# A graph network kernel on one core: TensorE's dense chunks also wait for GpSimd's gathers

## The chip, the core and the metric

One core of a Trainium2 chip. The metric is device microseconds of one execution; lower is better. The core's engines run their own instruction queues in order and meet only in semaphores: TensorE (PE) multiplies, VectorE (DVE) and ScalarE (ACT) work elementwise, GpSimd (POOL) here issues the gathers, SyncE (SP) and ScalarE issue the other transfers.

## What is computed

There are 6250 nodes with 64 features and 200,000 edges, sorted by destination, each with a source, one of 32 types and a weight. The first layer sends `x[src]` through one of 32 matrices that are mixed from 4 bases, scales by the edge's weight and sums by destination; then come a bias, relu, the addition of `x` and a layernorm. The second layer does nearly the same with one matrix, a self loop and a division by the summed weights.

```python
msg_b = jnp.einsum('ei,bio->ebo', h[src], weight)      # 4 bases
msg = jnp.einsum('ebo,eb->eo', msg_b, w_comp[etype]) * edge_norm[:, None]
x = layernorm(x + relu(segment_sum(msg, dst, N) + bias))
h = x @ W                                              # second layer
out = segment_sum(deg_inv[dst] * ew * h[src], dst, N)  # with loops of weight 1
x = layernorm(x + out + b)
```

## The kernel before

**Steps.** The edges are cut into 1563 chunks of 128. A *step* takes a group of 8 chunks; three steps (`U`) make an iteration, there are 65 iterations (`ITERS`), so 195 steps, and a tail of 3 chunks. All is unrolled on TensorE; on GpSimd it is a loop.

**First layer, in each step.** GpSimd issues one indirect transfer for each chunk (L824): 128 rows of `x`, one to a partition, into one of three buffers `gathered_rows`. In the function `gather_group` (L815) it first waits until ScalarE has written the group's indices (`idx_ready`) and counts `gathers_begun` up. ScalarE writes these indices (L927) when TensorE has read the rows that lay in the same buffer, so three steps back (`rows_read`). TensorE multiplies the rows with small factors (`sum_parts`, L1283), ScalarE copies the result (L985), and TensorE places it in a window of 44 nodes (L1296). Eight times in the first 20 iterations SP fetches the last chunk's rows instead of GpSimd, so there are 1559 gathers of `x`.

**Second layer, beside it.** The second layer isn't gathered. For each iteration of 24 chunks TensorE builds a *dense block*: how much each source node contributes to a window of destinations. `sum_chunk` (L1249) is one dense chunk: three matmuls of one-hot matrices with the "main" part (L1259) and three with the seam to the next chunk (L1269), into four banks in turn (`dense_ps`, `node_ps`, `types_ps`, `sums_ps`). It waits for VectorE's one-hots (`hots_ready`; made at L1886 to L1897) and for ScalarE's copies of the banks (`chunk_copied`, L1056), and it counts `dense_summed`. The blocks are stored in memory (SP, L733), come back when nodes of the first layer are finished (`load_unit`, L632), and TensorE applies them: to the last block at once (L1349), to earlier ones in "visits" (L1383), late ones in runs of three (L1406).

**TensorE's order in a step S**, from iteration 5 (L1480 on): dense chunks 0 and 1; the sum of the rows of step S-2, behind their landing (L1283); dense chunks 2, 3, 4; the placing of S-2 (L1296); dense chunks 5, 6, 7; in each third step the block products (L1349); the visits (L1383, none to six a step, more in later iterations); the coefficients for VectorE (L1244).

**What already holds GpSimd.** From iteration 8 on (step 24) a gather group is called with `behind_dense`. Then its third, fifth and seventh gather (`GATHERED_BEHIND = {2: 5, 4: 8, 6: 9}`) wait for dense chunks: for five of the step before, for all eight of it, and for the first of its own step. After each of these three waits GpSimd counts `gathers_paced` up. Both counts, `gathers_begun` and `gathers_paced`, are there before the change; nobody waits for them.

**After the loop** TensorE runs the last visits, some of which stand in its queue ahead of the last groups' sums, transforms the last batch of nodes and finishes the second layer (L1431), and the results are normalised and stored.

A second version of everything, for inputs that don't fit the planned order, is in the program and isn't run.

Of the kernel before, what the change touches and what calls it, by code (L numbers as in the profile page):

```python
# [36 lines left out]
U = 3  # L37
# [59 lines left out]
FETCHES = 4  # L97
# [114 lines left out]
def gnn_two_layers(nc, x, src, dst, etype, eweight, w0, w_comp, bias0, w1, bias1, out):  # L212
# [17 lines left out]
    with ctx:  # L230
# [158 lines left out]
        for u, (b, k, end, with_partial) in enumerate(UNITS):  # L389
            if u < BEGUN[-1]:  # L390
                step = next(n for n in range(ITERS * U) if BEGUN[n + 1] > u)
# [767 lines left out]
        def _(pe):  # L1159
# [77 lines left out]
            def look_up_coefs(step, s, chunks, count, halves=None):  # L1237
# [8 lines left out]
                if 4 * h + n == chunks:  # L1246
                    last.then_inc(coefs_ready, count)

            def sum_chunk(b, h, j):  # L1249

                n = b * DENSE + j
                pe.wait_ge(hots_ready, n + 2)
                if j == 0 and b:
                    pe.wait_ge(chunk_copied, n)
                values = NODES_OF[j] * TILES
                main = dense_ps[j % 4][:, 0:values]
                seam = dense_ps[(j + 1) % 4][:, 0:TILES]
                for w in range(3):
                    last = nc.tensor.matmul(main, lo_hot[:, w, j // 2, :, j % 2], node_hot[:, j // 2, 0:values, j % 2],  # L1259
                                            start=(j == 0 and w == 0), stop=(w == 2), skip_group_check=True)  # L1260
                    if w == 0 and (j == LAST_BANK or b == 0 and j < LAST_BANK):

                        nc.tensor.matmul(dense_ps[j % 4][:, values:values + TILES], no_node[:, :], no_node[:, 0:TILES],
                                         start=False, stop=True, skip_group_check=True)
                last.then_inc(dense_summed, 1)
                if j < DENSE - 1:
                    pe.wait_ge(chunk_copied, n + 1)
                    for w in range(3):
                        nc.tensor.matmul(seam, lo_hot[:, w, j // 2, :, j % 2], carry_hot[:, j // 2, :, j % 2],  # L1269
                                         start=(w == 0), stop=(w == 2), skip_group_check=True)  # L1270
# [163 lines left out]
            with pe.If(early == 1):  # L1434
# [42 lines left out]
                for i in range(FIRST_REGULAR, ITERS):  # L1477
# [3 lines left out]
                    for s in range(U):  # L1481
                        step = i * U + s
                        j0, of_last = DENSE_OF[s].start, divmod(step - 2, U)
                        mixed = i < MIXED_UNTIL
                        for j in range(j0, j0 + (1 if mixed else 2)):
                            sum_chunk(i, i, j)

                        if taken and s == 0:
                            pe.wait_ge(self_added, 2 * taken)
                        if turns is not None and s == 1:  # L1490
                            pe.wait_ge(nodes_read, turns + 1)
                        if turned is not None and s == 2:
                            pe.wait_ge(self_added, 2 * turned + 1)
                        if mixed:
                            for v in range(CH - 1):
                                between(i, s, v)
                                sum_chunk(i, i, j0 + v + 1)
                        else:
                            sum_rows(*of_last, step % 2)
                            for j in range(j0 + 2, j0 + 5):  # L1500
                                sum_chunk(i, i, j)
                            if i >= MANY_FROM:
                                pe.wait_ge(unit_added, BEGUN[step])
                            place(*of_last, step % 2)
                            for j in range(j0 + 5, j0 + CH):
                                sum_chunk(i, i, j)

                        use_coefs(step)
                        if s == 2 and tiles_done(i - 1):
                            pe.wait_ge(partial_taken, i)  # L1510
                        if s == 1 and tiles_done(i - 1):
                            apply_block(i - 1, i - 1)
                        for u in range(BEGUN[step], min(BEGUN[step] + VISITS_OF_COEFS, BEGUN[step + 1])):
                            sum_unit_of_block(u, visit_ps[u - BEGUN[step]])
                        if mixed:
                            look_up_coefs(step, s, CH, 1, [1])
                        else:
                            look_up(i, s)
                        if i >= MANY_FROM:
                            pe.wait_ge(window_added, step - 1 + FREE)  # L1520
                        for u in range(BEGUN[step] + VISITS_OF_COEFS, BEGUN[step + 1]):
                            sum_unit_of_block(u, visit_ps[u - BEGUN[step]])
                        if turns is not None and s == 0:
                            pe.wait_ge(window_added, (i - 1) * U + 1 + FREE)
                            transform(0, turns, parts_ps)
                        if turned is not None and s > 0:
                            turn_x1(turned, s - 1, parts_ps, 1)
# [873 lines left out]
```

## Time and profile before

| | us |
|---|---|
| median of 3 runs | 2767.2 |
| lowest, highest | 2765.88, 2772.87 |
| span of the profiled execution | 2042.2 |
| TensorE busy | 1497.4 |
| GpSimd busy | 1495.6 |
| VectorE busy | 1288.6 |
| ScalarE busy | 856.8 |

The span goes from the first to the last instruction of one profiled execution. The profiled execution's own time is not recorded; the median of the runs lies 725.0 us above its span. Busy times are by engine; matmuls overlap their weight loads.

### The profile page before, as it was taken

Reading aid. Unit: us, or ns where it says so; the run is one execution under the profiler, and the core shown is the slowest. Engines: PE = TensorE matmul, PEld = TensorE weight load, DVE = VectorE, ACT = ScalarE, POOL = GpSimd, SP = SyncE. Lnnn points to the kernel's source line nnn. Section 1 sums busy time; section 2 is a strip of 40 time slices with the busy share of each in tenths; the row PEclk is TensorE's granted clock in tenths of the full one; section 3 lists DMA queues with packets and bytes.
Section 4 is the critical chain, followed back from the end, with each engine's and each line's share of the span. In section 5 each row is a group of like instructions: output and inputs, shape, how many; then the busy total and the mean of one; then the engine's idle time right before and its main releaser. Section 6 shows DMA issues by size and latency. Waiting matters only on the chain.

```text
span 2042.2 us, 61156 instructions
## 1 busy us (share of the span) xinstructions
PE 1497.4 (73%) x21470; PEld 1196.1 (59%) x21470; DVE 1288.6 (63%) x3623; ACT 856.8 (42%) x2171; POOL 1495.6 (73%) x1590
## 2 busy tenths in 40 slices
PE   3785566655765776777677687778778788888986
PEld 2554444544554655566566566566667667677854
DVE  8886555756557555666655575565765656477647
ACT  5563343534444443444344344443444434344313
POOL 7777777777777777777777777777777777777750
PEclk7898777878787888888888898899999999899998
DMA  5544434434334455445444545554355554455695
GB/s 135 156 148 149 141 103 142 140 128 134 92 128 140 121 152 156 147 128 152 142 121 136 147 107 160 148 151 142 105 155 157 165 163 110 122 179 141 198 346 187
DMA packets 197569, 299.93 MB, mean 147 GB/s; under 512 B 66502, under 2 KB 137083, under 8 KB 191135
## 3 DMA queue, kind: packets, MB, share of 16 engines
q1 hardware_dynamic: 99496, 167.96, 23.3%
q0 software_dynamic: 50112, 51.41, 12.9%
q10 hardware_dynamic: 47671, 76.76, 12.4%
q8 instruction: 173, 2.83, 0.6%
q14 instruction: 117, 0.96, 0.1%
HBM read 187.43 MB, written 108.56 MB: 145 GB/s over the span
## 4 chain that ended last, share of the span: by engine, by line
PE 33%; POOL 29%; issue 19%; DMA 9%; DVE 3%; ACTq 3%; ACT 2%; DVEq 1%; POOLq 1%
POOL gathered_rows L824 29%; DMA gathered_rows<-in_x,idx 8%; PE coefs_ps L1383 4%; PE types_ps L1259 4%; PE coefs_ps L1349 3%; PE node_ps L1259 3%; PE sums_ps L1259 3%; PE sums_ps L1283 3%; PE dense_ps L1259 3%; PE sums_ps L1296 3%; ACTq L648 2%; ACT room L1056 1%; PE node_ps L1269 1%; PE sums_ps L1360 1%; PE coefs_ps L1244 1%
## 5 line engine op out<-in xcount | busy, mean ns | idle before, releaser
L824 POOL DMA_INDIRECT gathered_rows<-in_x,idx x1559 | 1475.7, 947 | 477.5 <-issue 426.7
L1283 PE MATMUL sums_ps<-gathered_rows,chunk_factors 128*32 128x64 f32 x3118 | 98.3, 253 | 407.0 <-DMA gathered_rows<-in_x,idx 218.7
L1897 DVE TENSOR_TENSOR first_room<-first_room,dve_ps 128x1024 bf16<-128x1024 bf16 x585 | 365.0, 679 | 0.0
L1283 PEld LDWEIGHTS sums_ps<-gathered_rows,chunk_factors 128*32 128x32 f32 x3118 | 63.1, 125 | 423.2 <-issue 208.6
L1056 ACT COPY room<-dense_ps 128x294 f32 x390 | 168.8, 433 | 332.1 <-PE dense_ps L1259 277.5
L985 ACT COPY parts<-sums_ps 128x128 f32<-128x128 f32 x196 | 52.0, 265 | 465.6 <-PE sums_ps L1283 462.3
L1919 DVE TENSOR_TENSOR dve_ps<-coefs_ps,edges 128x32 f32<-128x32 f32 x196 | 38.6, 197 | 330.7 <-PE coefs_ps L1244 326.2
L1259 PE MATMUL dense_ps<-first_room 128*128 128x245 bf16 x1170 | 219.2, 301 | 31.8 <-DVE first_room L1897 31.6
L1056 ACT COPY room<-node_ps 128x294 f32 x390 | 168.8, 433 | 168.1 <-PE node_ps L1259 61.8
L1891 DVE TENSOR_TENSOR first_room<-dve_ps,first_room 128x1960 bf16<-128x1960 f16 (+2 forms) x260 | 238.7, 939 | 0.0
L1259 PE MATMUL sums_ps<-first_room 128*128 128x245 bf16 (+1 forms) x1170 | 233.8, 312 | 0.0
L1259 PE MATMUL types_ps<-first_room 128*128 128x245 bf16 x1170 | 227.5, 311 | 0.0
L1259 PE MATMUL node_ps<-first_room 128*128 128x245 bf16 x1170 | 211.9, 293 | 0.0
L1056 ACT COPY room<-sums_ps 128x294 f32 (+1 forms) x390 | 171.4, 439 | 70.9 <-ACT room L1056 49.3
L1056 ACT COPY room<-types_ps 128x294 f32 x390 | 168.9, 433 | 69.5 <-ACT room L1056 47.0
L1976 DVE TENSOR_TENSOR acc_room<-acc_room,sums_ps 128x88 f32 x196 | 47.6, 243 | 238.1 <-PE sums_ps L1296 227.3
L1383 PE MATMUL coefs_ps<-acc_room,x_nodes 128*64 128x107 f32 x2742 | 170.6, 260 | 0.0
L1383 PEld LDWEIGHTS coefs_ps<-acc_room,x_nodes 128*64 128x64 f32 x2742 | 143.7, 136 | 15.3 <-issue 9.5
L1349 PE MATMUL coefs_ps<-room,x_nodes 128*64 128x107 f32 x2632 | 136.5, 258 | 7.5 <-ACT x_nodes L996 5.7
L1269 PEld LDWEIGHTS node_ps<-carry_hot,first_room 128*128 128x128 bf16 x1170 | 87.7, 106 | 87.1 <-ACT room L1056 70.9
L1269 PE MATMUL node_ps<-carry_hot,first_room 128*128 128x49 bf16 x1170 | 101.7, 196 | 46.2 <-ACT room L1056 45.0
L1886 DVE TENSOR_TENSOR first_room<-dve_ps,first_room 128x1024 bf16<-128x1024 f16 x195 | 133.1, 683 | 2.6 <-PE dense_ps L1259 1.4
(300 smaller groups left out, 2470.4 us busy)
## 6 DMA issues: line engine op xcount, KB each, us to landing
acc_room<-block_table ACTq DMA_DIRECT2D x147, 374.5 KB
block_table<-room SPq DMA_DIRECT2D x11, 2621.5 KB
type_rows<-in_edge_type SPq DMA_DIRECT2D x260, 96.0 KB
gathered_rows<-in_x,idx POOLq DMA_INDIRECT x1559
block_table<-room SPq DMA_DIRECT2D x9, 2247.0 KB
block_table<-room SPq DMA_DIRECT2D x9, 1872.5 KB
block_table<-room SPq DMA_DIRECT2D x10, 1498.0 KB
acc_room<-block_table ACTq DMA_DIRECT2D x43, 321.0 KB
```

Of the source, the lines that this page charges most:

```text
L824: pool.indirect_dma_start(gathered_rows[:, s, j, 0:D], None, rows, bass.IndirectOffsetOnAxis(ap=idx[:, s, j:j + 1], axis=0)).then_inc(rows ...
L985: nc.scalar.copy(parts[:, q, :, :], parts_ps[:, 0:QUADS * D].rearrange("p (k f) -> p k f", f=D)).then_inc(part_copied, count)
L1056: nc.scalar.copy(blocks_out[:, h % 2, :, bass.ds(offset, nodes)], dense_ps[j % 4][:, 0:nodes * TILES].rearrange("p (w h) -> p h w", h=TILE ...
L1259: last = nc.tensor.matmul(main, lo_hot[:, w, j // 2, :, j % 2], node_hot[:, j // 2, 0:values, j % 2], start=(j == 0 and w == 0), stop=(w = ...
L1269: nc.tensor.matmul(seam, lo_hot[:, w, j // 2, :, j % 2], carry_hot[:, j // 2, :, j % 2], start=(w == 0), stop=(w == 2), skip_group_check=True)
L1283: last = nc.tensor.matmul(parts_ps[lane:lane + LANE, D * k:D * k + D], chunk_factors[:, q, c, :], rows, start=True, stop=True)
L1296: last = nc.tensor.matmul(window_ps[D * h:D * h + D, 0:HALF * WIN], parts[:, q, k, :], places[:, q, k, HALF * h:HALF * h + HALF, :].rearra ...
L1349: last = nc.tensor.matmul(partial_ps[side:side + D, :], x_nodes[:, t, 1:D + 1], blocks_out[:, h % 2, t, :], start=(t < 2), stop=(t >= done ...
L1383: last = nc.tensor.matmul(to[side:side + D, :], x_nodes[:, FIRST_TILE[k] + t, 1:D + 1], tile_of(u, t), start=(not with_partial and t < 2), ...
L1886: nc.vector.tensor_tensor(lo_hot[:, 2, q0:q1, :, :], compared(P), keys(lo_key, P), ALU.is_equal).then_inc(lo_hots_ready, 1)
L1891: nc.vector.tensor_tensor(node_hot[:, a:e, 0:values, :], key_iota[:, 0:values, :].unsqueeze(1).to_broadcast([P, e - a, values, 2]), of_pai ...
L1897: last = nc.vector.tensor_tensor(lo_hot[:, w, q0:q1, :, :], lo_hot[:, 2, q0:q1, :, :], part_of_weights(w), ALU.mult)
```

## The change

Before each dense chunk, TensorE now also waits for GpSimd. `v` is the chunk's number in its step, and `step` in the new function is the step before the chunk's own. Chunks 0 and 1 wait until the gather group of the step before has been begun, chunks 2 and 3 until that group's third gather has been let go, chunks 4 and 5 until its fifth, chunks 6 and 7 until its seventh. This holds from step 25 on, since the counts of `gathers_paced` begin at step 24. GpSimd's own waits stay as they are.

```diff
+            def wait_for_gather(step, v):
+
+                if step >= 2 * FETCHES * U:
+                    if v > 1:
+                        pe.wait_ge(gathers_paced, 3 * (step - 2 * FETCHES * U) + v // 2)
+                    else:
+                        pe.wait_ge(gathers_begun, step + 1)
+
@@
                         mixed = i < MIXED_UNTIL
+
+                        def sum_behind(j):
+
+                            wait_for_gather(step - 1, j - j0)
+                            sum_chunk(i, i, j)
+
                         for j in range(j0, j0 + (1 if mixed else 2)):
-                            sum_chunk(i, i, j)
+                            sum_behind(j)
@@
                             sum_rows(*of_last, step % 2)
                             for j in range(j0 + 2, j0 + 5):
-                                sum_chunk(i, i, j)
+                                sum_behind(j)
                             if i >= MANY_FROM:
                                 pe.wait_ge(unit_added, BEGUN[step])
                             place(*of_last, step % 2)
                             for j in range(j0 + 5, j0 + CH):
-                                sum_chunk(i, i, j)
+                                sum_behind(j)
```

## Rows read from the trace of the kernel before

**Rows 1.** The page: span, PE, the gather, VectorE's hots.

```profile
span 2042.2 us, 61156 instructions
...
PE 1497.4 (73%) x21470; PEld 1196.1 (59%) x21470; DVE 1288.6 (63%) x3623; ACT 856.8 (42%) x2171; POOL 1495.6 (73%) x1590
...
L824 POOL DMA_INDIRECT gathered_rows<-in_x,idx x1559 | 1475.7, 947 | 477.5 <-issue 426.7
...
L1897 DVE TENSOR_TENSOR first_room<-first_room,dve_ps 128x1024 bf16<-128x1024 bf16 x585 | 365.0, 679 | 0.0
```

**Rows 2.** Stretches: length, busy us (instructions) by engine, clock, DMA share, GB/s.

```profile
240.00:560.00 320.00, 199.25 (x2635) 158.16 (x2636) 188.30 (x481) 131.82 (x345) 242.03 (x256) 0.78 0.41 127
...
1000.00:1500.00 500.00, 384.73 (x5706) 313.53 (x5707) 314.69 (x838) 211.93 (x540) 378.16 (x400) 0.88 0.48 138
1500.00:1960.00 460.00, 389.62 (x6404) 327.47 (x6401) 283.20 (x800) 186.52 (x478) 348.06 (x369) 0.96 0.55 161
```

**Rows 3.** Timeline of POOL: start, us, engine, line, instruction, [idle before <-releaser].

```profile
1004.96 0.94 POOL L824 DMA_INDIRECT gathered_rows<-in_x,idx  x1 [0.31 <-issue]
1006.21 0.95 POOL L824 DMA_INDIRECT gathered_rows<-in_x,idx  x1 [0.30 <-PE node_ps L1259]
...
1786.45 0.95 POOL L824 DMA_INDIRECT gathered_rows<-in_x,idx  x1 [0.30 <-issue]
```

**Rows 4.** Waits of POOL, 240 to 1960 us: total us, times, longest us.

```profile
POOL gathered_rows L824 <- issue: 371.5, 1219, 0.3
...
POOL gathered_rows L824 <- ACT idx L930: 4.3, 14, 0.3
```

**Rows 5.** All gathers of L824: ns min/median/max, then first and last start.

```profile
L824 POOL DMA_INDIRECT gathered_rows<-in_x,idx x1559: 940/944/2115, 8.9 to 1959.0; - x195
```

**Rows 6.** Waits of PE: 240-1700, 1700-1970, 1880-1965 us, whole span.

```profile
PE sums_ps L1283 <- issue: 185.4, 44, 8.5
PE sums_ps L1283 <- DMA gathered_rows<-in_x,idx: 167.0, 65, 10.0
...
PE sums_ps L1283 <- DMA gathered_rows<-in_x,idx: 8.4, 4, 5.0
...
PE sums_ps L1283 <- DMA gathered_rows<-in_x,idx: 6.7, 2, 5.0
...
PEld node_ps L1259 <- issue: 12.2, 62, 0.2
```

**Rows 7.** Timeline of PE: in steps 101, 102, 179 and at the end.

```profile
1008.72 0.50 PE L1259 MATMUL types_ps<-first_room 128*128 128x245 bf16 x3
...
1009.82 0.79 PE L1259 MATMUL dense_ps<-first_room 128*128 128x245 bf16 x3
...
1012.20 0.69 PE L1259 MATMUL types_ps<-first_room 128*128 128x245 bf16 x3
...
1019.83 0.65 PE L1283 MATMUL sums_ps<-gathered_rows,chunk_factors 128*32 128x64 f32 x16 [4.46 <-issue]
...
1798.60 0.43 PE L1283 MATMUL sums_ps<-gathered_rows,chunk_factors 128*32 128x64 f32 x16
1798.97 0.51 PE L1259 MATMUL types_ps<-first_room 128*128 128x245 bf16 x3
...
1799.39 0.49 PE L1259 MATMUL sums_ps<-first_room 128*128 128x245 bf16 x3
...
1961.33 0.50 PE L1283 MATMUL sums_ps<-gathered_rows,chunk_factors 128*32 128x64 f32 x16 [5.03 <-DMA gathered_rows<-in_x,idx]
1961.76 2.41 PE L1406 MATMUL node_ps<-room,x_nodes 128*64 128x321 f32 x8
...
1967.26 1.31 PE L1406 MATMUL dense_ps<-first_room,x_nodes 128*64 128x321 f32 x8
```

**Rows 8.** Chain of waits, near its end: start us, us, what.

```profile
1955.23 6.05 DMA gathered_rows<-in_x,idx
```

**Rows 9.** Core: span and mean granted clock.

```profile
core 0: 2042.2 us, clock 0.867
```

## Prediction

> **What bounds the kernel now.** I began with the page: span 2042.2 us [rows 1]. TensorE (PE) is busy 73% of it, and GpSimd (POOL) with its gathers alone, 1475.7 us, 72%, so the share decides nothing; the row of the gather has 1559 instructions of 947 ns, with 426.7 us of "issue" in front of them. Next the stretches [rows 2]: PE grows from 62% of the time (199.25 of 320) to 85% (389.62 of 460), while POOL is busy 75.6% in each. An engine that shows the same share beside light and heavy work of the others runs at its own cadence. Its timeline shows that cadence [rows 3]: 0.94 us of gather, 0.30 us of issue, one start each 1.25 us. The waits of POOL from 240 to 1960 us [rows 4] say the same: whoever is named as releaser (PE, ScalarE), no wait is over 0.3 us, and that is the cadence's own gap. The view of the gather's line has the first and last start of them all: the first gather starts at 8.9 us, the last at 1959.0 [rows 5]. 1558 intervals of 1.249 us (0.944 and 0.305 of issue; 371.5 / 1219, rows 4) are 1946 us; the stretch is 1950.1. So in the whole kernel POOL lost about 4 us to anybody. Lastly the chain [rows 8]: up to 1955 us it goes through the gathers, then 6.05 us until the last group of eight has landed, then TensorE's last units, to 2042.2. In short: **8.9 + 1950 us of gathers + 83 us after them**. TensorE isn't in the first two terms.
>
> The trace shows no time of its own for what lies around the span. The median of the runs is 2767.2, 725.0 above the span; I take that difference as constant, and the rivals hold the case that it isn't.
>
> **What TensorE does with its slack.** In a step PE sums eight dense chunks, and after the second of them the rows gathered two steps earlier (L1283). From 240 to 1700 us it waits for those rows 352 us (185.4 + 167.0), up to 10.0 us at a time; from 1700 to 1970 only 8.4 us [rows 6]. So late in the kernel PE works nearly without a pause, behind POOL, and there a delay of PE is not absorbed at once. Rows 7 show one step: POOL began the group of step 100 at 1006.21 [rows 3] after the last of step 99 at 1004.96, and when that had landed PE summed step 99; chunks 2, 4 and 6 of step 101 began at 1008.72, 1009.82 and 1012.20.
>
> **The change part by part.** It adds eight waits of PE in each step from 25 to 194, 170 steps, and nothing else: no instruction of POOL, VectorE, ScalarE or SP moves, no DMA. (a) Chunks 0 and 1 of a step wait until POOL has begun the group of the step before; (b) chunks 2 and 3, 4 and 5, 6 and 7 until POOL is at that group's third, fifth, seventh gather, so at 2.5, 5.0 and 7.5 us of its cadence.
>
> How long is PE held? In step 101 the group begins at 1006.21: chunk 2 may go from 1008.7 (it goes at 1008.72, no hold), chunk 4 from 1011.2 (it would go at 1009.82, held 1.4), chunk 6 from 1013.7 (it would go at 1012.20 + 1.4 = 13.6, held 0.1). Before the next sum, at 1019.83, PE stood 4.46 us; it now stands 1.5 us less. That is the effect in each light step: a piece of the long wait is cut off and put between the chunks. Done for all 170 steps, with each step's own chunk starts as rows 7 has them and everything behind a hold moved along, this gives about 215 us of holds in 283 places, in 124 of the steps, most under 1.4 us, paid out of the 352 us. I count this as zero on the path, since what hides it is PE's own wait for the same gathers.
>
> Behind the held chunk stand on PE: the other chunks, the place matmuls (L1296), the block products (L1349), the visits (L1383) and the coefficients (L1244). ScalarE waits for the chunks and, through rows_read, for L1283 before it writes the indices of a later group; VectorE waits for L1244; POOL waits for dense chunks. Does any of it reach POOL? POOL needs chunk 4 of step S-1 when it is at the third gather of S, and the indices of S, which need the sum of S-3. In the step where PE is furthest behind, 179, it sums the rows of 177 at 1798.60, 12.15 us after POOL began the group of 178 at 1786.45 [rows 3, 7]. The group of 180, which needs this sum for its indices, begins 20.0 us after 1786.45, and its third gather, which needs chunk 4 of step 179, comes at 22.5. Some 7 us are left; the holds carried into that step are 2.3 us. So POOL doesn't stop: **0 us**.
>
> Now the end. Holds in the late part: steps 162, 163, 166, 174, 175 and 189 by the same working, up to 2.4 us carried at once. The two waits for rows between 1880 and 1965 us sum to 6.7 us, 5.0 of it at the very end [rows 6]; the other, 1.7 us near 1900, eats most of that, and 0.9 us is left. PE comes to the sum of step 194 at 1956.3 and stands until 1961.33, 5.03 us [rows 7, 8]. 0.9 of 5.03 is gone and nothing moves: **0 us**. The upper bound of this term: all 2.4 us, still less than 5.03.
>
> The waits as instructions: the trace of before shows none alone. Lower bound 0: in step 179 a chunk follows the one before in 0.42 us (1798.97, 1799.39), with two waits in each, and no gap of PE is listed [rows 7]. Upper bound 0.2 us each, the longest "issue" idle that TensorE's weight loads have in front of a node_ps chunk [rows 6]. I take 0.02 us, nearest the dense stretch. From 1901 on PE has no wait for rows before the last sum: 4.5 steps of 8 waits are 36, so 0.7 us; with the holds 1.6 us of the 5.03. At 0.2 us it would be 7.2 + 0.9, so 3 us at the end, and more from the steps before (third rival).
>
> What comes back: at 1961.33 the clock fell for one stretch after the idle 5.03 us, and the eight matmuls of the unit behind it took 2.41 us, while a later unit of the same eight takes 1.31 [rows 7]. With a shorter idle piece it may stay up: 0 to -1.1 us. **Sum: 0 + 0 + 0, with -1.1 to +3 around it**, so a span of 2042 and a time of 2767.
>
> The granted clock deserves a word. Its mean is 0.867 [rows 9], and it is 0.78 in the lightest stretch, 0.96 in the heaviest [rows 2]; the same three matmuls of a chunk take 0.79 us at 1009.82 and 0.49 at 1799.39 [rows 7]. (0.133 × 2042 × 2 = 543 us at 1.2 GHz.) The Trainium skill, "TensorE: Matmul & The Clock Gate", section "HAM oscillation — how this bites in real kernels", says that a TensorE that waits long between bursts is slowed at each burst, and that one should keep the idle pieces short. The trace agrees, and by that rule alone the change is a good one: the clock goes up. It would be worth time where PE sets the end; by the rows that is nowhere before 1961 us.
>
> **Rivals.**
> (1) *Faster: PE is on the path in the timed executions.* The 725.0 us show in no view. The Trainium skill, "Runtime: NRT & Kernel Launch", section "The ~15µs preamble/postamble breakdown", puts 9 to 15 us around a kernel; by it some 700 us would be work that the timed executions do more slowly than this one, and its bound could be another. For it the rows have only the size of that difference; against it, one fixed piece explains it too. If PE were on the path in a tenth of the steps that are held, the regained clock, at most half of 543 us in all (272), gives 27 us: **2740**. In the profiled execution it could give the 1.1 us and the 4 us that POOL lost, no more.
> (2) *Slower: a gather and VectorE's wide operations exclude each other in the timed executions.* VectorE makes the hots in a burst each step, behind PE's chunks; L1897 is the largest part. Against: here gathers of 940 to 944 ns [rows 5] ran beside a VectorE that is busy 59 to 63% [rows 2]. For: 725 us over 1559 gathers are 0.47 us each, near what a wait for half an operation of 679 ns (L1897), 0.34, would be [rows 1]. The holds spread PE's chunks over the group and with them VectorE's hots; if one more gather in each of the 124 held steps meets an operation, 124 × 0.34 = 42 us, half of that if the bursts only shift: **2788**. [...]
> (3) *Slower: the waits cost PE, and PE is late at the end.* From 1700 to 1960 us, 26 steps, PE waits 8.4 us for rows [rows 6], so a step of its own takes (260 - 8.4) / 26 = 9.7 us, against POOL's 10.0. With 0.15 us × 8, three quarters of the bound, it is 10.9: 26 × 0.9 = 23 us behind, less the 5.03 at the end: **+18 us, 2785** (at 0.2 us +29). It decides from 0.06 us a wait, where 26 × (9.7 + 0.48 - 10) reaches the 5 us. For it: rows 6's 0.2. Against: the 0.42 us chunks.
> (4) *The waits are always met*, because PE is never early. In the light steps it is, by rows 6; if not, the time is the same, 2767.
>
> **How the numbers follow.** Forecast 0.57 and rival 4 0.03, both 2767 with a range of their own of 2762 to 2773; rival 1 0.20; rival 2 0.09; rival 3 0.11. A difference under 0.3%, 8.3 us, can't be told from no change. So faster 0.20, same 0.60, slower 0.20. The range, 2745 to 2790, holds the forecast and the greater part of both sides.
>
> **What would show it.** Right: gathers still 1559 at 1.249 us starts, POOL's waits at most 0.3, the last gather at 1959 ± 2; PE's waits for the gathered rows down from 352 us to about 140, new waits of up to 2.5 us at L1259 released by POOL; the clock of 240 to 1500 us up; PE still waiting at the last full sum. Wrong in the reason: a last gather later than 1963 (POOL was stopped), no idle at the last sum (PE late), or a time that moves while the span doesn't, which would mean that the 725 us aren't constant.

## The result

| set (one chip each) | kernel before, us | kernel after, us | after / before, 95% |
|---|---|---|---|
| first | 2765.97 (20 runs) | 2774.07 (20 runs) | 1.0028 [1.0014, 1.0041] |
| again, chip 3 | 2795.65 (18) | 2810.21 (6) | 1.0051 [1.0037, 1.0065] |
| again, chip 15 | 2047.70 (29) | 2047.43 (12) | 1.0000 [0.9989, 1.0011] |

The change makes the kernel slower by 8 to 15 us where an execution takes about 2770 to 2800 us, and does nothing where it takes about 2048 us. Executions of the same kernel are of these two kinds, below the long and the short kind. Every set was of one kind throughout: chips 8 and 15 gave the short one, chips 3 and 11 the long one, chip 11 twice; the first set's chip isn't known by number. So every ratio here is against the kernel before in the same set. The profile of before that the prediction was read from, with its span of 2042.2 us, was of the short kind; the times that stood beside it were of the long kind.

The page of the changed kernel in its first set, a long execution: span, busy times, chain, the gathers (columns as in [rows 1]).

```profile
span 2776.8 us, 62460 instructions
...
PE 1864.4 (67%) x21470; PEld 1371.6 (49%) x21470; DVE 1296.1 (47%) x3623; ACT 851.8 (31%) x2171; POOL 1492.5 (54%) x1590
...
PE 51%; another core or an unknown queue 17%; issue 16%; ACT 6%; DVE 5%; ACTq 4%; DVEq 1%; DMA 0%; SPq 0%
...
L824 POOL DMA_INDIRECT gathered_rows<-in_x,idx x1559 | 1472.5, 945 | 1196.6 <-issue 462.9
```

Read against [rows 1]: the gathers are as long as before (945 ns), but 1196.6 us of idle stand in front of them instead of 477.5, and the chain has no GpSimd in it at all. TensorE has it, and more than its 51%: the 17% of "another core or an unknown queue" (483 us) are waits for TensorE's own semaphores, all but 1.8 us (worked out from the semaphores of the waiting instructions), whose updates come too late for the view to link them. More on that in the last experiment. The execution's own time was 2778.62 us, 1.8 above its span: nothing of 725 us lies around a span. There are 1304 more instructions than in [rows 1] (61156).

Its stretches, columns as in [rows 2]:

```profile
240.00:560.00 320.00, 192.24 (x1975) 128.90 (x1974) 150.40 (x392) 101.95 (x268) 185.61 (x197) 0.72 0.32 105
1000.00:1500.00 500.00, 344.85 (x3957) 253.64 (x3956) 230.03 (x602) 158.46 (x406) 285.89 (x303) 0.78 0.37 107
1500.00:1960.00 460.00, 320.41 (x3942) 249.27 (x3942) 212.95 (x567) 140.41 (x359) 255.52 (x271) 0.81 0.36 103
```

The number of instructions done is what to look at: 303 on GpSimd in the 500 us where [rows 2] has 400, and 3957 matmuls where it has 5706. Its clock, its gathers and two waits of GpSimd (240 to 1960 us, as [rows 4]), then three of TensorE (240 to 1700 us, as [rows 6]), the first its longest:

```profile
core 0: 2776.8 us, clock 0.777
```

```profile
L824 POOL DMA_INDIRECT gathered_rows<-in_x,idx x1559: 938/944/1282, 9.5 to 2674.9; - x195
```

```profile
POOL gathered_rows L824 <- ACT idx L930: 131.8, 59, 4.7
POOL gathered_rows L824 <- PE node_ps L1267: 99.4, 42, 5.8
```

```profile
PE node_ps L1277 <- ACT room L1056: 122.3, 57, 6.7
PE sums_ps L1291 <- issue: 51.4, 88, 1.2
...
PE sums_ps L1291 <- ACT acc_room L1015: 13.2, 8, 5.5
```

GpSimd waits up to 5.8 us for TensorE's chunks and for indices, where [rows 4] had 0.3. TensorE's wait for landed rows, 167.0 us in [rows 6], is gone. So here TensorE sets the time, partly through the copies that ScalarE makes of its results (L1056), and GpSimd follows it.

Is that the change's doing? The kernel before, in a long execution of its own, says no:

```profile
span 2760.2 us, 61156 instructions
...
PE 1865.2 (68%) x21470; PEld 1364.2 (49%) x21470; DVE 1296.4 (47%) x3623; ACT 852.6 (31%) x2171; POOL 1493.3 (54%) x1590
...
PE 53%; another core or an unknown queue 19%; issue 15%; ACT 7%; ACTq 4%; DVE 3%; DVEq 0%; DMA 0%; SPq 0%
...
L824 POOL DMA_INDIRECT gathered_rows<-in_x,idx x1559 | 1473.4, 945 | 1179.2 <-issue 463.1
```

It is the same picture, 16.6 us shorter. Against the short execution of [rows 1] it is 718 us longer; TensorE is busy 368 us longer with the same 21470 matmuls (1865.2 against 1497.4, at a mean clock of 0.776 against 0.867), while VectorE and GpSimd are as busy as there. And the changed kernel in a short execution is the picture of the rows of before:

```profile
span 2048.0 us, 62460 instructions
...
PE 36%; POOL 25%; issue 18%; DMA 10%; DVE 4%; ACTq 3%; ACT 2%; SPq 1%; DVEq 1%; POOLq 1%
```

```profile
L824 POOL DMA_INDIRECT gathered_rows<-in_x,idx x1559: 940/944/2764, 9.5 to 1963.5; - x195
```

```profile
POOL gathered_rows L824 <- issue: 370.9, 1217, 0.3
...
POOL gathered_rows L824 <- ACT idx L930: 1.8, 6, 0.3
```

### The profile page after: what moved, and what is told of

Read it like the earlier page. It is cut to its first block, busy times and chain, and to the rows that moved or that the text cites. A ratio compares the mean times of both kernels' runs of the same rounds, so it can differ in the third digit from the quotient of the medians.

```text
span 2776.8 us, 62460 instructions
## 1 busy us (share of the span) xinstructions
PE 1864.4 (67%) x21470; PEld 1371.6 (49%) x21470; DVE 1296.1 (47%) x3623; ACT 851.8 (31%) x2171; POOL 1492.5 (54%) x1590
## 4 chain that ended last, share of the span: by engine, by line
PE 51%; another core or an unknown queue 17%; issue 16%; ACT 6%; DVE 5%; ACTq 4%; DVEq 1%; DMA 0%; SPq 0%
PE coefs_ps L1391 8%; PE coefs_ps L1357 7%; PE node_ps L1267 6%; PE types_ps L1267 5%; ACT room L1056 5%; PE sums_ps L1267 5%; PE dense_ps L1267 4%; PE sums_ps L1304 3%; PE sums_ps L1291 3%; PE node_ps L1277 2%; ACTq L648 2%; PE coefs_ps L1244 2%; PE sums_ps L1277 1%; DVE first_room L1911 1%
## 5 line engine op out<-in xcount | busy, mean ns | idle before, releaser
L824 POOL DMA_INDIRECT gathered_rows<-in_x,idx x1559 | 1472.5, 945 | 1196.6 <-issue 462.9
L1056 ACT COPY room<-dense_ps 128x294 f32 x390 | 168.7, 433 | 553.4 <-PE dense_ps L1267 266.3
L1391 PE MATMUL coefs_ps<-acc_room,x_nodes 128*64 128x107 f32 x2742 | 251.3, 314 | 54.5 <-issue 53.0
L1267 PE MATMUL sums_ps<-first_room 128*128 128x245 bf16 (+1 forms) x1170 | 261.4, 336 | 27.0 <-issue 26.2
L1056 ACT COPY room<-node_ps 128x294 f32 x390 | 168.2, 431 | 352.3 <-remote 195.0
L1267 PE MATMUL dense_ps<-first_room 128*128 128x245 bf16 x1170 | 238.4, 315 | 54.2 <-issue 44.9
L1056 ACT COPY room<-sums_ps 128x294 f32 (+1 forms) x390 | 170.9, 438 | 300.9 <-remote 129.3
L1357 PE MATMUL coefs_ps<-room,x_nodes 128*64 128x107 f32 x2632 | 205.8, 313 | 79.4 <-issue 58.6
L1267 PE MATMUL types_ps<-first_room 128*128 128x245 bf16 x1170 | 243.3, 324 | 9.1 <-issue 8.6
L1391 PEld LDWEIGHTS coefs_ps<-acc_room,x_nodes 128*64 128x64 f32 x2742 | 200.2, 172 | 92.6 <-issue 88.0
L1267 PE MATMUL node_ps<-first_room 128*128 128x245 bf16 x1170 | 240.5, 323 | 4.9 <-issue 4.9
L1056 ACT COPY room<-types_ps 128x294 f32 x390 | 168.5, 432 | 213.7 <-remote 89.6
L1357 PEld LDWEIGHTS coefs_ps<-room,x_nodes 128*64 128x64 f32 x2632 | 180.0, 176 | 94.8 <-issue 91.7
L1291 PE MATMUL sums_ps<-gathered_rows,chunk_factors 128*32 128x64 f32 x3118 | 133.0, 254 | 89.3 <-issue 69.7
L1277 PE MATMUL sums_ps<-carry_hot,first_room 128*128 128x49 bf16 x1170 | 109.4, 204 | 109.5 <-issue 59.2
L1277 PEld LDWEIGHTS sums_ps<-carry_hot,first_room 128*128 128x128 bf16 x1170 | 97.3, 113 | 157.7 <-issue 83.2
```

The costliest lines, as they stand in the source:

```text
L824: pool.indirect_dma_start(gathered_rows[:, s, j, 0:D], None, rows, bass.IndirectOffsetOnAxis(ap=idx[:, s, j:j + 1], axis=0)).then_inc(rows ...
L1056: nc.scalar.copy(blocks_out[:, h % 2, :, bass.ds(offset, nodes)], dense_ps[j % 4][:, 0:nodes * TILES].rearrange("p (w h) -> p h w", h=TILE ...
L1291: last = nc.tensor.matmul(parts_ps[lane:lane + LANE, D * k:D * k + D], chunk_factors[:, q, c, :], rows, start=True, stop=True)
L1357: last = nc.tensor.matmul(partial_ps[side:side + D, :], x_nodes[:, t, 1:D + 1], blocks_out[:, h % 2, t, :], start=(t < 2), stop=(t >= done ...
L1391: last = nc.tensor.matmul(to[side:side + D, :], x_nodes[:, FIRST_TILE[k] + t, 1:D + 1], tile_of(u, t), start=(not with_partial and t < 2), ...
```

## The experiments

Kernels of one set ran on one chip; "before" is each set's own. Medians in us.

### Is the wait held, or only there?

> The kernel before, unchanged. Theory A (the trace of 2042.2 us is of an execution unlike the timed ones, and TensorE is on the path in those): the profile shows a span near 2764 us, TensorE stalls in streams without waits as in the trace after (455 of them, 365 us), POOL idle some 1190 us, a chunk 2 that starts 18 us or more behind the begin of the matching group. Theory B (only the kernel after has this): a span near 2042 again beside times near 2766. Ratio 1.000 within its interval.

> The same eight waits in a step, each asked of a group two steps older, so that none can hold TensorE where the change's doesn't. Theory A1 (in the timed executions no wait is ever unmet, and what costs is only the instruction in TensorE's queue): as the changed kernel, +5 to +11 us over before (ratio 1.002 to 1.004). Theory A2 (the waits hold TensorE at moments that one profile doesn't show): back to the time before, ratio 1.000 ± 0.001.

```diff
-pe.wait_ge(gathers_paced, 3 * (step - 24) + v // 2)
+pe.wait_ge(gathers_paced, 3 * (step - 24) + v // 2 - 6)   # two groups older
-pe.wait_ge(gathers_begun, step + 1)
+pe.wait_ge(gathers_begun, step + 1 - 2)
```

> Only the waits of chunks 0 and 1 (a quarter of the waits). A1: a quarter of the cost, +2 us (1.0007). A2, if the pairs from the third gather on are what holds: 1.000; if the first two are, 1.003.

```diff
-if step >= 24:
+if step >= 24 and v < 2:      # chunks 0 and 1 only
```

> The changed kernel with eight more waits before each chunk, all met long before (64 more in a step). A1, at 6 ns a wait (8.1 us / 1304 more instructions): 10900 more waits, +65 us (1.026); half of it if two waits share an instruction. A2: no more than the changed kernel, 1.003.

```diff
+for back in range(1, 9):      # eight more waits a chunk, all met
+    pe.wait_ge(gathers_begun, step + 1 - back)
```

These four ran in the short kind, before at 2047.95: the kernel before once more 1.0007 [0.9998, 1.0016], waits_past 1.0003 [0.9992, 1.0015], first_two 1.0009 [0.9998, 1.0019], many_waits 1.0022 [1.0010, 1.0034] with 6744 more instructions than before. What was expected of the first four had been meant for the long kind, so they say only that the effect is gone in a short execution. The one interval above 1, of many_waits, is 4.5 us over 6744 instructions, 0.7 ns each. The second set made it firm:

> The changed kernel again. If the execution is of the kind of the trace before (span near 2045), theory A (the change costs only where TensorE is on the path) expects ratio 1.000 ± 0.001 here, with some 150 to 215 us less of waiting at the sum of gathered rows; theory C (the change costs the same 8 us in any execution) 1.004. If it is of the other kind (span near 2770): 1.002 to 1.004 by both, and none of the 1360 waits unmet.

> The changed kernel with eight more waits before each chunk (5440 more instructions in TensorE's queue than the changed kernel, 6744 more than before). In an execution near 2048 us: as measured, +2 to +7 us. In one near 2767 us, theory A1 (what costs is the instruction, 8.1 us / 1304 = 6 ns each): +42 us, ratio 1.015; theory A2 (the waits' effect on the order of the work): as the changed kernel, 1.003.

> One look at the kernel before. Theory A: in an execution near 2767 us its trace has the same stalls of TensorE inside streams without a wait as the changed kernel's (some 450 of them, 365 us) and POOL idle some 1190 us; in one near 2048 us, none.

Change 1.0000 [0.9989, 1.0011], many_again 1.0007 [0.9997, 1.0016]. The short execution of the changed kernel shows TensorE's waits from 240 to 1700 us:

```profile
PE sums_ps L1291 <- issue: 180.4, 40, 8.2
PE sums_ps L1291 <- DMA gathered_rows<-in_x,idx: 162.0, 63, 8.5
PE dense_ps L1267 <- DVE first_room L1911: 7.2, 4, 3.1
PE dense_ps L1267 <- issue: 6.6, 6, 2.1
```

342 us of waits for rows, where [rows 6] has 352, and at the chunk's line L1267 nothing that GpSimd released. The prediction had 140 us and new waits of 1 to 2.5 us. Nothing is held. The reason is in the events of GpSimd's own queue in this execution (worked out over all groups from step 24 on): it raises `gathers_begun` a median of 15.2 us before the group's first gather starts, and `gathers_paced` 15.2 us before the third, fifth and seventh. That is 12 gathers of 1.25 us. A dense chunk starts 7.5 us or more after the count that it waits for. Against the gather itself 739 of the 1360 chunks are early, by up to 5 us: so the prediction saw rightly that TensorE runs ahead of the gathers, but the counts run further ahead. The Trainium skill, "TensorE: Matmul & The Clock Gate", section "Architectural detail: the array is 16× 32×32, not 1× 128×128", gives GpSimd's engine a queue eight deep. An estimate from it, eight gathers of 1.25 us, is a count 10 us ahead; the trace's 15.2 us decide. By either the holds vanish, since no chunk was more than 5 us early.

### What do the waits cost where the time is long?

> The changed kernel once more, for which kind of execution this chip gives. Near 2048 us: 1.000 ± 0.001 as before. Near 2767 us, theory A: 1.002 to 1.004.

> Chunks 0 and 1 of each step from 25 on wait until the rows that TensorE sums behind them have landed, so that they are really held by gathers (in the traces so far the counts are raised 12 gathers ahead of the gather, and no wait of the change is unmet). In an execution near 2048 us, theory D (TensorE's slack hides a real hold, as the prediction had it): ratio 1.000 ± 0.001, L1259 instead of L1283 stands behind the landing, 0.85 us moved behind it in each light step. Theory E (a held TensorE comes late to the end): 1.001 to 1.003, +2 to +6 us.

```diff
+if v < 2:     # instead of the change's waits; S is the chunk's step
+    pe.wait_ge(rows_gathered[(S - 2) % U], ...)   # the group of S-2 has landed
```

> Chunks 5, 6 and 7 of each step wait until the gathers of the step before have landed, 11 us after they were begun: a hold of 5 to 6 us in each light step. Theory D: the holds are paid out of the wait for rows until the last 100 us; there TensorE comes some 8 us late to the last sums, less the 5.0 it had: +3 us (1.0015), and POOL still without a wait over 0.3 us. Theory E: the work behind the hold no longer fits in a step's 10.0 us in the late iterations, POOL is held in turn, +20 us or more (1.01).

```diff
+if v > 4:     # chunks 5 to 7, instead of the change's waits
+    pe.wait_ge(rows_gathered[(S - 1) % U], ...)   # the group of S-1 has landed
```

> The changed kernel with 24 more waits before each chunk, all met, some 96 to 128 instructions of 51 ns more in a step, 5 to 6.5 us of TensorE's queue. In an execution near 2048 us, if such instructions are hidden behind matmuls: 1.003. If TensorE's queue is what becomes late: 26 late steps of 9.7 + up to 6 us against 10.0, +100 us (1.05), and POOL's waits over 0.3 us for dense chunks. Near 2767 us, at the 6 ns of theory A1: +110 us.

```diff
-for back in range(1, 9):
+for back in range(1, 25):     # 24 more waits a chunk on top of the change's
```

> The eight waits with values two groups older, the same 1304 instructions. Near 2048 us: 1.000 ± 0.001. Near 2780 us, theory A1 (the instructions are the cost): as the change, 1.002 to 1.006. Theory A2 (the values matter): 1.000 ± 0.001.

> 6744 more instructions in TensorE's queue than before. Near 2048 us: 1.000 to 1.003. Near 2780 us, at the 6 to 11 ns for each that the change showed: +42 to +74 us (1.015 to 1.027); at the 28 ns of the kernel with 17624 more (497 us): +190 us (1.07); if there is a threshold between, as the change: 1.005.

> The kernel before, one look. Near 2780 us: TensorE's stalls inside streams without waits as in the changed kernel (440 to 470 of them, some 365 us), POOL's gathers held some 1190 us in all. Near 2048 us: none of either.

All these fell in the long kind, on two chips:

| kernel | instructions added | ratio, 95% | us | ns each |
|---|---|---|---|---|
| held_two | 284 | 1.0009 [0.9996, 1.0022] | 2.5 | 9 |
| held_three | 510 | 1.0035 [1.0021, 1.0049] | 9.8 | 19 |
| the change, first set | 1304 | 1.0028 [1.0014, 1.0041] | 7.7 | 6 |
| the change (after_third) | 1304 | 1.0051 [1.0037, 1.0065] | 14.3 | 11 |
| waits_past_2 | 1304 | 1.0026 [1.0003, 1.0048] | 7.2 | 6 |
| many_third | 6744 | 1.0228 [1.0200, 1.0256] | 63 | 9 |
| flood | 17624 | 1.1784 [1.1763, 1.1805] | 499 | 28 |

Waits whose values are two groups old, and so can hold nothing, cost what the change costs, within wide intervals. Eight further waits a chunk that are always met cost in proportion. A wait by itself isn't an instruction; a second one on an instruction that has one already (a chunk's first matmul waits for hots) becomes an instruction of its own in TensorE's queue (2363 of these there instead of 1059, each 51 ns in the trace), of which 6 to 11 ns come out in the time. The 28 ns of the flood are another regime: 17624 instructions of 51 ns are 899 us of TensorE's queue, they stand in its trace as idle "issue" before the chunks (253.9 us before `types_ps` alone) and its clock is 0.634, so its slope isn't used. Two more rows of its waits:

```profile
PE sums_ps L1269 <- POOLq L819: 54.3, 58, 2.3
PE dense_ps L1269 <- POOLq L819: 24.0, 28, 1.3
```

They look like holds by GpSimd's count ("POOLq" as releaser) and aren't: in the flood no chunk of steps 25 to 194 starts less than 18.4 us after the count that the change asks for. Some later count was raised while TensorE stood, and the view took it for the releaser; waits_past_2, whose waits can hold nothing, has 3.8 us of such rows. In the changed kernel's long execution there is one, 0.5 us in one place, where no chunk starts less than 11.6 us after its count:

```profile
PE sums_ps L1267 <- POOLq L823: 0.5, 1, 0.5
```

held_two and held_three were meant to hold TensorE for landed rows. In the long kind TensorE comes too late for that (its waits show none for a gather at the chunks), so they test little but their 284 and 510 instructions; held_three's 19 ns each (12 to 27 by its interval) lies a little above the others, and why stays open. So no run here held a chunk for a gather, and what such a hold would cost in the short kind isn't known.

### The waits without their instructions, and instructions taken out

> The change's waits, with the same counts and the same values, stand on the second of a chunk's three main matmuls instead of the first, where they are the only wait and need no instruction of their own. A (what costs is the 1304 added instructions in TensorE's queue, 6 to 11 ns each, where TensorE sets the time): where executions are of the 2767 us kind 1.000, between 0.999 and 1.0015, against 1.0026 to 1.0051 of the change; where they are of the 2048 us kind 1.000 too. B (what costs is that a wait on GpSimd's counts now and then holds TensorE): as the change, 1.0025 to 1.005 in the 2767 us kind.

```diff
 for w in range(3):            # the chunk's main matmuls
+    if w == 1 and paced:
+        wait_for_gather(*paced)   # was ahead of the first
```

> The kernel before with four of its own waits in each step (for the factors and the copied part of the sum of the gathered rows, for the place operand and the added window of the placing) moved a little ahead, onto single matmuls of a dense chunk that have no wait, so that no instructions of their own are needed for them; the values are the same. A (instructions in TensorE's queue cost 6 to 11 ns each in the 2767 us kind): some 500 to 700 fewer, so 3 to 8 us less, 0.997 to 0.999; in the 2048 us kind 1.000. B (they cost nothing, the chunk's place does): 1.000 in both, or above where the earlier place makes TensorE wait for ScalarE or VectorE.

```diff
+    if w and len(riding) >= w:
+        pe.wait_ge(*riding[w - 1])
@@ sum_parts
-    pe.wait_ge(factors_ready, step + 2)
-    pe.wait_ge(part_copied, step + 1)   # now on chunk 1's second and third matmul
@@ place_parts
-    pe.wait_ge(place_ready, step + 2)
-    pe.wait_ge(window_added, step + FREE)   # now on chunk 4's
```

Before stood at 2802.66. **riding: 2802.11, 1.0001 [0.9989, 1.0014]**, with the change's every wait, and 61156 instructions as before. Its interval lies wholly below after_third's, whose waits have the same counts and values, and meets the first set's [1.0014, 1.0041] only at its end. The change itself wasn't timed in this set. With waits_past_2 (old values, same cost) and many_third (more instructions, more cost) it says that the waits' coupling to GpSimd is free, and that the instructions are the loss.

**lean: 2794.01, 0.9978 [0.9964, 0.9992]**, 60796 instructions, 360 fewer (500 to 700 had been expected). It is faster than the kernel before, by little but clear of the noise. 6.2 us over 360 are 17 ns each, 6 to 28 by the interval: the sign was foretold, and the size fits the low end only, so some of it may come from where the waits stand. It was timed in the long kind alone.

### Is GpSimd ever the bound in a long execution?

> The kernel before without GpSimd's own waits for dense chunks (the gathers wait for their indices alone; nothing else is changed). In an execution near 2048 us, where no wait of POOL is over 0.3 us: 1.000. In one near 2767 us: 1.000 ± 0.002 if TensorE is the bound there, since gathers would only run further ahead; more than 1.003 if gathers that run ahead disturb TensorE or VectorE.

> The kernel before without GpSimd's waits for dense chunks, again, looked at in the 2767 us kind of execution. A (there TensorE's queue sets the time and GpSimd runs behind it): 1.000, between 0.998 and 1.002. B (there GpSimd's gathers are held by the dense chunks and carry the time): below 0.995. In the 2048 us kind, as measured already, 0.9992.

```diff
 if behind_dense and j in GATHERED_BEHIND:
-    pool.wait_ge(dense_summed, ...)     # before, without the change
```

In the short kind 2045.92, 0.9992 [0.9983, 1.0001]. In the long kind **3124.04, 1.1144 [1.1117, 1.1171]**: both theories of no_pace_2 missed it. The first expectation, of no_pace, had named it (gathers that run ahead disturb TensorE), without a size. Taking GpSimd's waits away makes GpSimd, and everything, later:

```profile
span 3126.8 us, 60643 instructions
...
PE 2019.9 (65%) x21470; PEld 1459.5 (47%) x21470; DVE 1287.1 (41%) x3623; ACT 854.0 (27%) x2171; POOL 1497.0 (48%) x1590
...
PE 54%; issue 27%; another core or an unknown queue 9%; DVE 5%; ACT 2%; ACTq 2%; DVEq 1%; DMA 0%; SPq 0%
```

```profile
POOL gathered_rows L823 <- ACT idx L929: 1125.9, 192, 26.6
```

GpSimd now runs its eight gathers in one go and then stands for the indices, 5.9 us a step. The timeline of TensorE and GpSimd shows what happens to TensorE beside such a run (start, us, engine, line, instruction, idle before):

```profile
1506.77 0.95 POOL L823 DMA_INDIRECT gathered_rows<-in_x,idx  x1 [3.82 <-ACT idx L929]
...
1509.95 1.34 PE L1348 MATMUL coefs_ps<-room,x_nodes 128*64 128x107 f32 x16
1510.52 0.94 POOL L823 DMA_INDIRECT gathered_rows<-in_x,idx  x1 [0.30 <-issue]
1511.77 0.94 POOL L823 DMA_INDIRECT gathered_rows<-in_x,idx  x1 [0.30 <-issue]
1512.48 0.34 PE L1348 MATMUL coefs_ps<-room,x_nodes 128*64 128x107 f32 x2 [1.19 <-issue]
...
1513.94 0.42 PE L1348 MATMUL coefs_ps<-room,x_nodes 128*64 128x107 f32 x4 [1.11 <-issue]
...
1515.37 0.40 PE L1348 MATMUL coefs_ps<-room,x_nodes 128*64 128x107 f32 x2 [1.01 <-issue]
1515.52 0.94 POOL L823 DMA_INDIRECT gathered_rows<-in_x,idx  x1 [0.30 <-issue]
1516.80 0.34 PE L1348 MATMUL coefs_ps<-room,x_nodes 128*64 128x107 f32 x1 [1.03 <-issue]
1517.51 2.12 PE L1348 MATMUL coefs_ps<-room,x_nodes 128*64 128x107 f32 x16 [0.37 <-issue]
```

These 41 block products have no wait between them. The first 16 run at full pace beside the third and fourth gather of the group; then TensorE does one to four and stands over 1 us, again and again, until the eighth gather (1515.52) is through. In a short execution of the changed kernel, with GpSimd's gathers 1.25 us apart without any pause, the same 41 take one row:

```profile
1065.60 2.11 PE L1357 MATMUL coefs_ps<-room,x_nodes 128*64 128x107 f32 x41
```

The changed kernel's long execution has the same thing, in milder form, because GpSimd there rests for dense chunks:

```profile
1423.21 0.94 POOL L824 DMA_INDIRECT gathered_rows<-in_x,idx  x1 [2.26 <-PE types_ps L1267]
...
1425.79 0.65 PE L1357 MATMUL coefs_ps<-room,x_nodes 128*64 128x107 f32 x9
...
1426.96 0.95 POOL L824 DMA_INDIRECT gathered_rows<-in_x,idx  x1 [0.30 <-issue]
1427.48 0.31 PE L1357 MATMUL coefs_ps<-room,x_nodes 128*64 128x107 f32 x2 [1.04 <-issue]
...
1429.46 0.94 POOL L824 DMA_INDIRECT gathered_rows<-in_x,idx  x1 [0.30 <-issue]
...
1431.75 2.47 PE L1357 MATMUL coefs_ps<-room,x_nodes 128*64 128x107 f32 x25 [1.09 <-issue]
```

Counted over each whole trace: places where TensorE stands over 0.35 us, as the views list idle time, between two matmuls of the same line and tiles with no wait on the second; and the share of time lost so while the nth gather of an unbroken run (starts under 1.4 us apart) is under way.

| execution | places | us | gathers 1 and 2 | 3rd | 4th | 5th and 6th |
|---|---|---|---|---|---|---|
| change, short | 0 | 0 | 0 | 0 | 0 | 0 |
| before, long | 339 | 232.7 | 2% | 2% | 10% | 28% |
| change, long | 341 | 241.8 | 1% | 2% | 11% | 30% |
| no_pace_2, long | 818 | 611.4 | 1% | 2% | 29% | 42% |

What is left falls shortly behind a run. In the time in which no gather has started for 2.8 us (300, 310 and 847 us of the three long executions) such stalls sum to 0, 0 and 0.05 us. So they are tied to gathers in flight, above all from the fourth of an unbroken run on, and only in the long kind. no_pace_2 makes the runs longer on purpose, and nothing else: the stalls grow by some 380 us and the time by 321. The landing isn't slower there: a group's rows are there 2.5 us after the start of its last gather in the median, against 2.9 us in the short kind.

The same gathers do a second thing, which the stalls don't count. TensorE's own updates of its semaphores come late. Here the sum of gathered rows has its last matmul at 1023.85 us, TensorE goes on with other chunks, but its update of `rows_read` comes only at 1027.46, 2.0 us after the start of the last gather of the run, and lets go ScalarE's copy (the kernel before, long):

```profile
1021.75 0.94 POOL L824 DMA_INDIRECT gathered_rows<-in_x,idx  x1 [2.32 <-remote]
...
1023.19 0.66 PE L1283 MATMUL sums_ps<-gathered_rows,chunk_factors 128*32 128x64 f32 x16
...
1025.50 0.94 POOL L824 DMA_INDIRECT gathered_rows<-in_x,idx  x1 [0.30 <-issue]
...
1027.48 0.27 ACT L985 COPY parts<-sums_ps 128x128 f32<-128x128 f32 x1 [4.18 <-remote]
```

Of the 1560 updates of `dense_summed` 533 are over 1.5 us behind the end that the trace gives the chunk's last main matmul (median 0.86 us); in the short executions 4 or 5 (0.01 us). Of the 148 with no gather started in the 2.8 us before, none is late. As the ends of matmuls are modelled, this can mean late ends or late updates; for who waits it is the same. It is what "remote" and "another core or an unknown queue" stand for here: in the chain of the kernel before 517 us, all waits for TensorE's semaphores.

That TensorE's instructions come late is not borne out as the reason for its stalls: the trace shows no transfer of instructions from 1508.6 to 1520 us of no_pace_2, across the stalls shown, and those of 16 KB took a median of 1.05 us for the kernel before in both kinds. Why one chip has this and another doesn't, and through what a gather reaches TensorE, no run shows.

## Why the prediction was wrong

Forecast: 2767.0, no change, with 0.20 on slower. Measured: slower by 0.28%, 2774.07, inside 2745 to 2790. That the time fell inside the range is luck: it was added up from stretches that no timed execution had. And the line that the prediction drew for "can't be told from no change", 0.3%, was too coarse; 20 runs each told 0.13%.

1. **"I take that difference as constant"** (the 725.0 us above the span). This step failed first. The timed executions were of the long kind, where the sum 8.9 + 1950 + 83 does not hold: the last gather starts at 2674.9 instead of 1959.0, and TensorE, not GpSimd, ends the chain. All of the "hidden beside GpSimd" that follows was true for the profiled execution and for no timed one. That the trace and the times could be of different kinds was visible from one number, 725 us; rival 1 named it.
2. **"0 us, since what hides it is PE's own wait"** for 215 us of holds in 283 places. The holds don't exist, in either kind of execution: GpSimd's queue raises its counts 15.2 us ahead of its gathers in the short one; in the long one TensorE's chunks start 11.6 us or more behind the counts. Rival 4 ("the waits are always met"), given 0.03, is what the traces show, though not by its reason: in the short kind TensorE is early. "The clock of 240 to 1500 us up" fell with it: 0.80 and 0.88 in the short execution against 0.78 and 0.88.
3. **"The waits as instructions ... 0.02 us"**, hidden up to the end. This is the term that the measured 8 us sit in, and the prediction had it at 0 on the path. Its lower bound rests on a misreading: the two waits of a chunk stand on two different matmuls, and so need no instruction, while the change's is a second one on the first. Its 1360 waits became 1304 instructions, each 51 ns in the trace. In the short kind they cost nothing that can be told, as argued. In the long kind many_third's 9 ns each would make 12 us of them, between the 7.7 and the 14.3 measured. The size taken, 20 ns, was of the right order; what was missed is that the cost applies to all of them and not to the last 36.
4. **The rivals.** Rival 1's premise held (TensorE on the path in the timed executions), its effect did not: with no holds there is no clock to win back. Rival 3 had the mechanism and the sign (the waits cost PE) and too late a place: it let the cost count only at the end, from 0.06 us a wait. It gave 2785 and 0.11. Rival 2 fell for the operations it named: the gathers are 944 ns in both kinds, beside a VectorE that is busy 47 and 63%, and of 1678 gathers beside L1897, in four traces of the kernel before, none took over 1 us. But those operations have one input in `dve_ps`, which is in PSUM. Beside operations with both inputs in SBUF gathers do get longer: 14 of 30 beside L1849 and 12 of 27 beside L2077 took over 1 us. There are 18 such gathers in 1559 in [rows 5]'s trace, the longest 2.1 us; what they take over 944 ns sums to the 4.0 us that GpSimd lost there.
5. **Right, for the short kind**: 1559 gathers 1.25 us apart (SP fetches the rows of four of the 1563 chunks, in iterations 7, 11, 15 and 19, not of eight), GpSimd's waits at most 0.3 us, TensorE still standing at the last full sum, 4.99 us where [rows 7] has 5.03. The last gather starts at 1963.5 where the prediction had 1959 ± 2, and took anything over 1963 for a stopped GpSimd; yet no wait of GpSimd is over 0.3 us. Kernels with added waits gave 1960.2 to 1964.8, the kernel before 1959.0 to 1959.6 in three traces; where these 4 us come from stays open, and the times don't show them:

```profile
1965.20 0.66 PE L1291 MATMUL sums_ps<-gathered_rows,chunk_factors 128*32 128x64 f32 x16 [4.99 <-DMA gathered_rows<-in_x,idx]
```

## What to carry to other kernels

Before a path is read from a trace, compare the profiled execution's own time with the timed ones: when they differ by a quarter, the trace is of another regime, and the question is which engine bounds in the one that is timed. A wait that is always met is free only when it is an instruction's only one; as a second wait it is an instruction, and on the engine that sets the time some 1300 of them cost 8 to 15 us here: put it on a neighbour that has none (riding, 1.0001), and do the same with old ones (lean, 0.9978). A count that GpSimd raises between its indirect transfers says that its queue got there, not that the transfer has begun: in the short kind it was 12 gathers early, in the long kind 0.8 to 2.1 us (medians). And a releaser in a view is an inference: "remote" was TensorE itself here, and "POOLq" nobody.

## What the runs showed of the hardware

- Two kinds of execution of one kernel, each chip known by number with one of them: 2048 us and 2767 to 2803 us, with the same busy times on VectorE and GpSimd, and 368 us more on TensorE. Even one chip of the long kind gave 2766.88 and 2802.66 for the kernel before in two sets, so only ratios within a set count there.
- In the long kind indirect gathers in flight stop TensorE's stream, over 1 us at a time in the rows shown (28% of the time of the fifth and sixth of an unbroken run, 42% without pauses), and make its semaphore updates late (533 of 1560 by over 1.5 us; none with no gather started in the last 2.8 us). The waits that hold GpSimd for dense chunks, worth nothing in the short kind (0.9992 without them), are worth 11% in the long one. Whether still shorter runs would win more wasn't tried.
- In both kinds a gather gets longer beside VectorE operations with both inputs in SBUF (14 of 30 beside L1849 over 1 us) and never did beside L1897, which has one in PSUM (0 of 1678).
